# Nine makes of a voting slot: two row-group patterns for the same nine matrix products

## The reference

```python
patches = extract_patches(x, 3, 3, STRIDE, PAD)      # 9 taps, 32 channels = 4 capsules of 8
priors  = einsum('nfdhwij,ofijud->nhwofiju', patches, weight)   # votes of 36 inputs for 4 outputs
logits  = zeros_like(priors)
for r in range(3):
    probs = softmax(logits, axis=-3)                  # over the 4 output capsules
    out   = sum(probs * priors, axis=-2)
    if r != 2:
        out    = squash(out)
        logits = logits + sum(priors * out, axis=-1)  # agreement of each vote with the output
out = squash(out)
```

## Time and profile before

| | us |
|---|---|
| median of 3 runs (lowest to highest) | 12900.15 (12896.17 to 12911.73) |
| the profiled execution | 12904.24 |
| its span, first to last instruction | 12902.4 |
| PE busy in it | 12303.8 (95%) |
| DVE / ACT / POOL busy | 9188.1 / 7592.3 / 3414.9 |

### The profile page before, as it was taken

The page is one execution under the profiler, slowest core; times in us unless marked ns, Lnnn a source line. Parts: engine busy times, 40 slices in busy tenths (PEclk is TensorE's granted clock), DMA queues, the critical chain, the costliest instruction groups (busy, mean ns, idle before and its releaser), DMA issues. The chain is left out here.

```text
span 12902.4 us, 255523 instructions
## 1 busy us (share of the span) xinstructions
PE 12303.8 (95%) x73276; PEld 4675.7 (36%) x73276; DVE 9188.1 (71%) x17067; ACT 7592.3 (59%) x15286; POOL 3414.9 (26%) x3268
## 2 busy tenths in 40 slices
PE   6999999999993799999999999999999999999899
PEld 2333333333331233333333333333333333333233
DVE  6777777777776677777777777777777777777311
ACT  4666666666663366666666666666666666666411
POOL 4777777767772000000000000000000000000143
PEclk9999999999996799999999999999999999999999
DMA  3111111101104332232232232232232233232255
GB/s 78 22 20 18 22 19 19 22 17 21 22 15 131 74 72 67 68 73 67 67 74 67 66 75 67 66 75 67 65 75 68 65 74 69 65 73 68 68 122 111
DMA packets 853483, 772.61 MB, mean 60 GB/s; under 512 B 587092, under 2 KB 621492, under 8 KB 840884
## 3 DMA queue, kind: packets, MB, share of 16 engines
q1 hardware_dynamic: 850612, 747.43, 25.5%
q10 hardware_dynamic: 1536, 8.39, 0.3%
HBM read 510.63 MB, written 244.96 MB: 59 GB/s over the span
## 5 line engine op out<-in xcount | busy, mean ns | idle before, releaser
L1547 DVE TENSOR_REDUCE a_big<-a_mp 128x1 f32<-128x512 f32 x8192 | 5219.2, 684 | 1826.1 <-PE a_mp L1381 1807.4
L1467 ACT ACTIVATE a_ex<-a_sc 128x512 f32<-128x512 f32 x8192 | 4426.3, 601 | 1935.5 <-PE a_sc L1369 1930.6
L1381 PE MATMUL a_mp<-a_ks,a_qs 108*128 108x512 bf16 x8192 | 3131.1, 383 | 39.7 <-DMA a_ks<-qk_parts 24.9
L1369 PE MATMUL a_sc<-a_qs,a_ks 111*128 111x512 bf16 x8192 | 3124.5, 383 | 6.8 <-ACT a_ex L1467 4.5
L893 DVE TENSOR_TENSOR r_prod<-r_pg,r_win 128x512 f32<-128x512 f32 x2816 | 1846.1, 683 | 783.2 <-PE r_pg L618 438.6
L546 POOL TENSOR_TENSOR r_prod<-r_temp,r_win 128x512 f32<-128x512 f32 x1792 | 2095.8, 1189 | 1158.9 <-ACT r_temp L845 954.5
L1283 POOL TENSOR_TENSOR a_pieces<-a_left,a_pieces 128x512 bf16<-128x512 f32 x256 | 295.5, 1154 | 7323.9 <-ACT a_pieces L1453 7323.9
L1395 PE MATMUL a_po<-a_ex,a_va 128*32 128x512 f32 x16384 | 2182.0, 605 | 1.6 <-ACT a_oc L1473 0.9
L1369 PEld LDWEIGHTS a_sc<-a_qs,a_ks 111*128 111x128 bf16 x8192 | 794.9, 97 | 2477.4 <-ACT a_ex L1467 1767.8
L1381 PEld LDWEIGHTS a_mp<-a_ks,a_qs 108*128 108x128 bf16 x8192 | 803.1, 98 | 914.1 <-DVE a_big L1547 238.3
L845 ACT COPY r_temp<-r_pg 128x512 f32<-128x512 f32 x1792 | 975.3, 590 | 77.2 <-PE r_pg L618 38.6
(11 more groups left out here) (185 smaller groups left out, 11641.8 us busy)
## 6 DMA issues: line engine op xcount, KB each, us to landing
a_qs<-qk_parts SPq DMA_DIRECT2D x768, 144.0 KB
a_ks<-qk_parts SPq DMA_DIRECT2D x768, 144.0 KB
qk_parts<-a_pieces SPq DMA_DIRECT2D x128, 768.0 KB, 5.2
f_t<-mixed SPq DMA_DIRECT2D x48, 1536.0 KB, 16.6
a_tw<-second SPq DMA_DIRECT2D x512, 128.0 KB, 3.0
mixed<-a_t SPq DMA_DIRECT2D x256, 256.0 KB, 2.1
r_win<-first SPq DMA_DIRECT2D x128, 280.5 KB, 4.9
a_zw<-layered SPq DMA_DIRECT2D x192, 144.0 KB, 12.0
```

Source lines behind the costliest of these rows:

```text
L1369: pe.matmul(sc[k % BANKS][:, :], ks[0:KROWS + NPART, p.h, head, 128 * kb:128 * kb + 128], qs[0:KROWS + NPART, p.h, head, CHUNK * qb:CHUNK ...
L1381: pe.matmul(mp[k % BANKS][:, :], qs[0:KROWS, p.h, head, 128 * q:128 * q + 128], ks[0:KROWS, p.h, head, CHUNK * half:CHUNK * half + CHUNK], ...
L1467: nc.scalar.activation(ex[:, k % RING, :], sc[k % BANKS][:, :], ACT.Exp, scale=scale).then_inc(exped.sem, 1)
L1547: nc.vector.tensor_reduce(big[:, x % 2, k // 2:k // 2 + 1], mp[k % BANKS][:, :], AX_X, ALU.max).then_inc(maxed.sem, 1)
```

## The change

Only PE's `make` and `slot` in the routing change, and only for voting slots.

```diff
             if voting:
-                q = slice(32 * (pos % 4), 32 * (pos % 4) + 32)
+                q = slice(32 * (pos % 3), 32 * (pos % 3) + 32)
                 last = pe.matmul(bank[:, :], wv[q, 128 * tap:128 * tap + 128], stack[q, lane, :],
-                                 start=True, stop=True, tile_position=(32 * (pos % 4), 0))
+                                 start=True, stop=True, tile_position=(32 * (pos % 3), 0))
...
-            for pos in range(4):
+            voting = s % 8 < LANES
+            for pos in range(3 if voting else 4):
                 if heavy:
                     make(p.n, s, pos)
             for x in back[:1]:
...
             for x in back[1:] + turn:
                 light(p, x, which)
-            for pos in range(4, 8):
+            for pos in range(3, 6) if voting else range(4, 8):
                 if heavy:
                     make(p.n, s, pos)
             for x in front:
                 sum_uniform(p, x)
             for x in front[:1]:
                 light(p, x, which)
-            for pos in range(8, 9):
+            for pos in range(6, 9) if voting else range(8, 9):
                 if heavy:
                     make(p.n, s, pos)
```

## The result

The changed kernel takes 13169.8 us (median of 4 runs, 13165.6 to 13173.8), the kernel before 12900.5 beside it (4 runs): 269.3 us more, a ratio of 1.0211, 95% interval [1.0198, 1.0224]. The prediction was 13168, with a range of 13030 to 13290. The profiled execution took 13165.6, its span 13162.7.

What follows compares the result with a forecast made beforehand. PE sets the routing's pace, through its loop with DVE. Per pass, 12.22 us of added waits less 3.86 removed gives +8.36; times 32 passes, +268 us, so 13168 from the median, range 13030 to 13290.

Steps and rivals of the forecast that it cites:

- Three runs cost PE what 4 + 4 + 1 cost: PE in voting slots: a run of four costs 1.07 us, of one 1.05, so the change saves nothing there.
- The long runs go: PE in five of eight voting slots: runs longer than 1.14 us hold 3.86 us a pass of removable waits.
- DVE's light starts a run later: DVE in voting slots: position 6 now comes behind the front; PE's ninth batch can start 4.68 us after the third run.
- Position 8's wait: PE in slots 3 and 11: position 8 waits 0.26 us for position 3's bank.
- slots 3 and 11: PE's ninth batch waits 1.56 us and position 8 0.26: added 1.8 us each, nothing removed.
- Slots 4 and 12: Slots one behind, not voting: first run to ninth batch grows from 1.47 to 2.37 us, added 0.9 each.
- the sign that I named: PE's ninth batch (line 656) waiting for DVE's product: from 0.2 to about 1.5 us in slots 4, 12, 3, 11.
- Slots 2 and 10: Ninth batch waits 1.0 or 0.97 us, then position 5 waits for ACT: net +1.5 in slot 2, +1.0 in 10.
- Slots 0, 1, 8 and 9: Waits mostly on ACT's late copies: net -0.2 us in slot 0, +0.9 in 1, -0.55 in 8, +0.4 in 9.
- Rival 3: Routing: ACT catches up within a slot, leaving DVE's waits alone, about 4.5 us net a pass, 13045; chance 0.17.
- Rival 1: Routing: the runs stop waiting and DVE keeps up, 3.86 us a pass saved, 12780; chance 0.08.
- Rival 5: PE in voting slots: more waits drop the clock to the 1.2 GHz level, 1700 us more, 14900; chance 0.02.

Runs made afterwards that it cites:

- Experiment 1: The changed kernel with row groups pos mod 4 instead of pos mod 3, runs of three kept: 13167.1 us, ratio 1.0212.
- experiment 2: The kernel before, with its runs of 4, 4 and 1, but on row groups pos mod 3: 13193.3 us, ratio 1.0234.
- (4): The changed kernel with runs of 3, 4 and 2 on four groups, position 6 made ahead of the front again: 13001.1 us, ratio 1.0079.
- experiment 5: The changed kernel with DVE multiplying only positions below 6 ahead of its light in voting slots: 13015.9 us, ratio 1.0102.
- experiments 6 and 10: 6: changed kernel, DVE's position 7 product done twice in voting slots, 13421.9 us; 10: kernel before, three runs in slots 0 and 8 alone, 12933.6 us.
- experiment 8: The changed kernel with half of position 7's product (256 of 512 columns) done a second time in voting slots: 13298.0 us, ratio 1.0313.
- the dose: The changed kernel with DVE's product of position 7 done a second time in voting slots, into an unread tile: 13421.9 us, ratio 1.0403.

## Why the prediction was right

- *Three runs cost PE what 4 + 4 + 1 cost.* Right: 1.07 for a run of three. Experiment 1 adds that the groups are indifferent to it, experiment 2 that four makes on three groups are not.
- *The long runs go.* Right for slots 0, 8 and 10 in size: the three slots came out within 0.12 of their sums. In slot 8 the run shrank from 2.45 to 1.83, as said, for position 5 still waits.
- *DVE's light starts a run later.* Right, and shown from both ends: a make put back (4) and the light put first (5) each give back over half. The predicted 4.68 from the third run was 4.56, since position 6's product came 1.16 behind the start of its run (2139.45 to 2140.61); the 1.29 of the row before was that of position 5, the second make of its run, and position 6 is now the first. Position 8's wait was 0.14, not 0.26 (a run of 1.27 less 1.13), for the same reason. So slots 3 and 11 added 1.57, not 1.8: the one term over-sized, 0.5 a pass together.
- *Slots 4 and 12.* 0.90 each as worked out: first run to ninth batch 2.36 (2149.77 to 2152.13) against 2.37. But the sign that I named, some 1.5 us of wait at line 656, came in slots 3 and 11 (1.37) and not in slots 4 and 12: there it is 0.21, against 0.20 before. The time lies in the first run, 2.16 instead of 1.26, whose fourth make goes into the bank of position 7.
- *Slots 2 and 10.* The sums fit (1.57 against 1.5, 1.12 against 1.0), the place does not. I had the ninth batch wait behind a back that is hidden, and position 5 behind ACT. The back itself waits, 1.46, since it writes the bank that DVE's subtraction still reads; its 0.59 then lies behind the wait and not beside it. That gave ACT the time to be ready: the second run of slot 10 is 1.14. Two errors of about 0.5 met.
- *Slots 0, 1, 8 and 9.* Right within 0.1 each, but the waits on ACT that I took for a lateness of ACT's own are DVE's light again, as experiments 6 and 10 show. Rival 3, in which ACT catches up, had therefore nothing to stand on.
- *Rival 1* missed that the chain, not the load, decides: DVE is idle for more time than before, and PE still waits. *Rival 5*, the clock, did not come, but I set it aside on a false reading: the mean of 0.99 does not show that the clock stays behind a wait of 1.35, for behind that very wait it fell in 15 of the 32 passes before. That it stayed behind the waits which the change adds (but for one slot) was luck. With some 0.35 us more in each of them (experiment 8) it begins to count.
- *Two sums* do not come out of the terms listed: slot 9's parts make 0.95, not 1.04, and rival 3's net is 3.75 a pass by the waits on DVE alone, or 4.9 with the waits left in slots 0 and 8, not 4.5. Neither moves the forecast by more than 3 us.

The total, 268 for 268, is thus closer than the parts: an over-sized term of some 0.5 a pass in slots 3 and 11 against some 0.2 too little in slots 2 and 10 and 0.2 in slot 6, which is the clock's and which I had at nothing. That they cancel is luck.

## What to carry to other kernels

Before makes or loads are regrouped, read the order of their consumer: a result that the consumer takes up early must not be issued late, and the room to look for is the slack of the chain from the issue to the wait that holds the issuing queue (0 to 0.3 us here), not the idle share of the consumer (23%). A wait that is removed at one bank of a ring comes back at the next bank or the next slot unless what fills it late is removed too, so an edit that helps a slot is worth what the two slots together show. And where the waits of TensorE grow, read its granted clock beside them, slot by slot and not as a mean: the dose cost 252 us where the chain alone explains 154, and a mean of 0.99 hid a fall in half the passes.

## What the runs showed of the hardware

- Two makes on one row group in a run of four: 1.91 us instead of 1.07. Three on three groups: 1.07.
- A product of the first make of a run started 1.16 behind the run (slot 10), one of the second make 1.29; in slot 9 I saw 1.24 for a first make (2131.08 to 2132.32), which I can't explain.
- Behind waits of 1.83 and 2.13 us PE ran at a granted clock of 0.53 in the stretches shown; the waits of up to 1.53 that the change adds left the routing's mean at 0.99. The length of the wait does not settle it alone: behind slot 6's wait of 1.25 to 1.36 the clock fell in 15 of 32 passes before and 20 after.
- DVE's small squash operations stretch: the operation of line 917 took 0.17 us in one slot and 0.72 in the next of the kernel of experiment 5. The trace divides it by POOL: 0.17 to 0.20 us in all 225 cases beside an idle POOL, 0.46 to 0.72 in all 63 beside a busy one. No run changes POOL's work to test it.
